# A two-layer transformer kernel on one core: the order of the value projection and of the query and key projections inside an attention slot

## The chip, the cores and the metric

The kernel runs on one core of one Trainium2 chip. The metric is device time in microseconds (us) of the whole program, lower is better. Engines are called PE (TensorE), DVE (VectorE), ACT (ScalarE), POOL (GpSimd) and SP (SyncE, which here only issues DMAs).

## The reference, cut to what matters

Eight sequences of 512 tokens with 256 features go through four blocks, each followed by a residual sum and a layer norm. The change touches only the first block's code; the routing part of the second runs in the same slots.

```
x = norm(x + attention_0(x))    # 16 heads of 16, softmax over keys j >= i
x = norm(x + experts_0(x))      # top 2 of 8, 7 experts of 512 slots, one no-op
x = norm(x + attention_1(x))    # rms norm, rotary, sigmoid weights divided by their sum
x = norm(x + experts_1(x))      # top 2 of 12, 8 experts of width 512, 4 that pass x on

# attention_0
q, k, v = split(x @ w_qkv + b_qkv)
s = where(j >= i, (q @ k.T) * 0.25, -inf)
out = softmax(s) @ v @ w_out + b_out
# experts_0, routing
w = softmax(x @ router_w.T + router_b); top 2; rank of each token in its expert, first 512 kept
```

## The kernel before, in words

The program has five stages: attention and routing of layer 0 (functions a_sp, a_pe, a_act, a_dve, a_pool), the experts of layer 0, attention and routing of layer 1, the experts of layer 1, and the last norm. A stage of attention is a software pipeline over the eight sequences. It is cut into ten slots, called zeroth, first, second, body (five times), seventh, eighth and ninth. In a body slot s the projections of sequence s+1 are made, the values and the row maxima of sequence s, the attention of sequence s-1, and output projection, norm and routing of sequence s-2.

A slot is a list of small steps, made once by `spread_out` at build time. Every engine walks the same list in order and does its own part of each step, and semaphores join them. So the list is the order of the instructions on every queue, SP's and POOL's too. The steps that matter here:

- `st n`, `av n` (20 each): scores of one unit (PE), exp (ACT, L834), mask of diagonal units (POOL, affine select, L1161), weights times values (PE, L719). `oe`, `on` (4 each): the accumulator is copied (ACT), transposed (PE, L729), and divided by the sum of the weights into o_nat (DVE, L909 and L911).
- `mx n` (40): PE makes scores again in bf16 (L810) and DVE takes their row maxima (L1093). `mc` splits 32 maxima into three bf16 parts (DVE, L1104 to L1108), `mr` turns them (PE, L819), `ms` stores them as three more rows of Q (SP, L667). `mc 0`, `mr 0`, `ms 0` stand in the middle of a slot, `mc 1` at its end, and `mr 1`, `ms 1` for it near the start of the next slot. Scores of the second half (`st 10`) wait for `ms 1`.
- `oT` (2): PE transposes o_nat (L737), ACT copies. `y` (2): output projection (PE, L745), residual sum (DVE, L921). `ln` (23 pieces): layer norm of y into x_out (DVE). `rT`, `lg`: PE transposes x_out (L755) and makes the router's logits (L762).
- `l1` (3 pieces), `l2` (22), `l3` (11): the routing, small DVE operations of 4 to 64 columns, each of which waits for the one before it. The first of l2 is L1004. `ps`: two small matmuls between l2 and l3. `sc` (8): POOL scatters the rows of x_out by indirect DMA (L1171).
- `qk n` (4): query and key projection of 128 columns for the next sequence. PE makes it (L793), ACT copies it twice out of the bank (L856, L861). `qs n`: DVE subtracts and casts (L1069, L1072), POOL subtracts once more (L1149), SP writes the three bf16 parts to DRAM (L650). `st_q 0` and `st_q 1` (SP, L603 and L607) load them back, stacked, for the first and the second eight heads. mx 0 of the next slot waits for the first stack, mx 20 for the second. qk come in the order 0, 2, 1, 3, where 0 and 2 belong to the first stack.
- `v n` (2): value projection of sequence s (PE, L800), bias and store by DVE (L1077). `xt` loads the transposed rows of sequence s+1 into the tile that v reads, and waits for v 1.

Three PSUM banks ("shared") are handed out in turn to every step of the list among xT, qk, ro, v, on, oT, y, rT, lg, ps, mx, mr (`bank_keys`). A step on PE therefore waits until the bank used three such steps before has been read, by DVE or by ACT.

How the list comes about: `evenly` merges two lists, the maxima and `rest`, so that both advance alike by the weights in WEIGHT (mx 0.9, v, y and qk 1.5, qs 0.8, rT 0.6, ln and each routing piece 0.25). Then the loop at the end of `spread_out` spreads the merged list over the st and av steps by the same weights. `("space", 0)` entries weigh 0.3 and vanish later.

## Time and profile before

| | us |
|---|---|
| median of 3 runs | 1785.55 |
| lowest, highest | 1783.24, 1787.79 |
| the profiled execution, its own time | 1787.79 |
| its span in the trace | 1786.0 |
| busy PE, DVE, ACT, POOL | 1456.3, 965.4, 694.6, 498.1 |
| mean granted clock of PE | 0.89 of full |

Busy times are sums over an engine's instructions. PE's includes time at the low clock. The body slots of layer 0 lie between about 147 and 492 us of the span, each between one oT 0 and the next.

### The profile page before, as it was taken

The numbers are of one execution on the slowest core, as the hardware profiler recorded it, in microseconds if no ns is written. First come the engines' busy times: TensorE is split into PE (matmuls) and PEld (weight loads), VectorE is DVE, ScalarE is ACT, GpSimd is POOL, SyncE is SP. The second block draws the span as 40 slices with busy tenths as digits, with TensorE's granted clock in tenths as the row PEclk, the third lists the DMA queues.
The fourth block names the chain that finished last, engine by engine and source line by source line (L and its number), as shares of the span: only waits on it lengthen the run. The fifth ranks groups of instructions, "written<-read, shape, count | busy, mean of one in ns | idle before, by whom it ended". The sixth has DMA issues, their size and how long they took to land.

```text
span 1786.0 us, 31302 instructions
## 1 busy us (share of the span) xinstructions
PE 1456.3 (82%) x10329; PEld 962.5 (54%) x10330; DVE 965.4 (54%) x3689; ACT 694.6 (39%) x957; POOL 498.1 (28%) x422
## 2 busy tenths in 40 slices
PE   3698898898798649999469999999998539999970
PEld 1245454454454426666235555565555429999970
DVE  3667778878866411111367776866653434444424
ACT  1153444454445311111045666666576312222222
POOL 4022233333334212121111132122212144444430
PEclk7798899999978669999689999999999769999995
DMA  6754336336333043432154534643635324444448
GB/s 160 195 115 88 83 92 141 88 92 137 87 61 107 13 160 86 127 95 59 35 119 99 107 77 105 132 110 71 128 84 146 133 75 72 71 71 71 69 82 250
DMA packets 122239, 182.88 MB, mean 102 GB/s; under 512 B 17112, under 2 KB 104562, under 8 KB 114433
## 3 DMA queue, kind: packets, MB, share of 16 engines
q1 hardware_dynamic: 98336, 151.84, 34.2%
q0 software_dynamic: 21504, 27.76, 9.6%
q10 hardware_dynamic: 2272, 1.67, 0.3%
q8 instruction: 70, 1.15, 0.3%
q14 instruction: 57, 0.46, 0.1%
HBM read 111.47 MB, written 77.02 MB: 106 GB/s over the span
## 4 chain that ended last, share of the span: by engine, by line
PE 57%; DVE 19%; issue 6%; DMA 5%; ACT 3%; POOL 1%; SPq 1%; DVEq 0%; ACTq 0%; POOLq 0%
PE ST L1795 7%; PE shared L1807 7%; PE ST L701 6%; PE OT L719 6%; PE ST L1261 6%; DVE scratch L1093 5%; PE shared L745 4%; PE OT L1269 3%; PE shared L1269 3%; PE shared L1456 2%; DMA x_in<-sum 2%; PE shared L793 2%; PE shared L810 2%; PE shared L762 2%; PE shared L737 2%
## 5 line engine op out<-in xcount | busy, mean ns | idle before, releaser
L834 ACT ACTIVATE arena<-ST 128x1024 f32<-128x1024 f32 x416 | 414.8, 1024 | 272.6 <-PE ST L701 267.4
L1093 DVE CUSTOM_DVE_ANT_0 scratch<-shared,mask 128x512 bf16<-128x512 f32 (+3 forms) x512 | 229.8, 486 | 92.6 <-PE shared L810 71.3
L701 PE MATMUL ST<-arena 96*128 96x256 bf16 (+2 forms) x1792 | 251.8, 277 | 15.3 <-DMA arena<-qk_parts 14.1
L719 PE MATMUL OT<-arena,v_aug 128*32 128x256 f32 (+1 forms) x3584 | 252.0, 383 | 4.1 <-POOL arena L1161 2.4
L701 PEld LDWEIGHTS ST<-arena 96*128 96x128 bf16 (+1 forms) x1792 | 159.9, 102 | 116.0 <-issue 50.6
L810 PE MATMUL shared<-arena 96*128 96x512 bf16 (+3 forms) x512 | 126.2, 322 | 52.7 <-DMA arena<-qk_parts 22.2
L1904 POOL DMA_INDIRECT sum<-arena,block_to_row x72 | 111.3, 1546 | 169.4 <-ACT arena L1858 157.8
L719 PEld LDWEIGHTS OT<-arena,v_aug 128*32 128x32 f32 x3584 | 85.1, 111 | 118.1 <-issue 66.4
L1161 POOL TENSOR_SCALAR_AFFINE_SELECT arena<-arena 128x512 f32<-128x512 f32 (+1 forms) x96 | 78.9, 822 | 226.0 <-ACT arena L834 226.0
L1807 PE MATMUL shared<-arena 128*128 x576 | 136.1, 379 | 0.0
L1636 POOL DMA_INDIRECT slot_x<-x_out,row_to x64 | 63.7, 995 | 177.0 <-DVE keep L1549 159.9
L810 PEld LDWEIGHTS shared<-arena 96*128 96x128 bf16 x512 | 43.4, 102 | 128.5 <-issue 65.1
L1807 PEld LDWEIGHTS shared<-arena 128*128 128x128 f32 x576 | 103.9, 190 | 11.2
L1621 POOL TENSOR_TENSOR qk_src<-qk_rest,qk_src 128x512 bf16<-128x512 f32 x32 | 37.7, 1178 | 252.0 <-DVE qk_src L1590 252.0
L1261 PE MATMUL ST<-arena 128*128 128x512 f32 x224 | 99.5, 603 | 5.1 <-ACT arena L1280 5.1
L1872 DVE COPY arena<-shared 128x256 f32<-128x256 f32 x72 | 30.5, 424 | 117.0 <-PE shared L1785 117.0
L1324 POOL DMA_INDIRECT sum<-arena,b_to x28 | 43.2, 1544 | 179.5 <-DVE arena L1307 151.6
L793 PE MATMUL shared<-xT,w_qkv 128*128 128x512 f32 x128 | 71.9, 694 | 24.7 <-DMA xT<-in_xT 14.6
L1290 DVE TENSOR_SCALAR arena<-ST 128x512 f32<-128x512 f32 x28 | 19.4, 691 | 111.2 <-PE ST L1261 111.2
L1171 POOL DMA_INDIRECT slot_x<-x_out,row_to x64 | 62.6, 979 | 50.3 <-DVE row_to L970 32.5
L1858 ACT ACTIVATE arena<-shared,block_gain 128x256 f32<-128x256 f32 x72 | 34.1, 474 | 106.4 <-PE shared L1807 106.4
L1852 ACT ACTIVATE arena<-ST 128x512 f32<-128x512 f32 x71 | 42.4, 597 | 84.7 <-PE ST L1795 84.7
(208 smaller groups left out, 2394.1 us busy)
## 6 DMA issues: line engine op xcount, KB each, us to landing
arena<-qk_parts SPq DMA_DIRECT2D x224, 128.0 KB, 7.2
qk_parts<-qk_src SPq DMA_DIRECT2D x64, 384.0 KB, 2.6
arena<-qk_parts SPq DMA_DIRECT2D x32, 384.0 KB, 4.6
block_rows<-slot_x SPq DMA_DIRECT2D x72, 130.0 KB, 2.2
arena<-qk_parts SPq DMA_DIRECT2D x32, 256.0 KB, 5.4
sum<-x_out SPq DMA_DIRECT2D x16, 512.0 KB, 2.9
arena<-in_experts_inter SPq DMA_DIRECT2D x7, 1024.0 KB, 5.2
arena<-in_experts_out SPq DMA_DIRECT2D x7, 1024.0 KB, 9.4
```

The costliest lines, as they stand in the source:

```text
L701: mm = pe.matmul(ST[n % 2][:, i * 256 + at:i * 256 + at + nq], K[par][0:rows, h, kb * P:(kb + 1) * P], Q[par][0:rows, h, q0:q0 + nq], star ...
L719: mm = pe.matmul(OT[32 * i:32 * i + 32, q0:q0 + nq], v_aug[par][:, kb, g * GH + i, :], PT[n % RING][:, i, at:at + nq], start=(u == 0), sto ...
L793: mm = pe.matmul(bank[:, :], w_qkv[:, c, n * P:(n + 1) * P], xT[:, c, :], start=(c == 0), stop=(c == CD - 1))
L810: mm = pe.matmul(bank[:, at:at + S - qb * P], Q[par][0:SK, head, qb * P:(qb + 1) * P], K[par][0:SK, head, qb * P:S], start=True, stop=True)
L834: act.activation(PT[n % RING][:, :, :], ST[n % 2][:, :].rearrange("p (h n) -> p h n", h=GH), func, scale=ATT_SCALE).then_inc(L["exp"], 1)
L1093: taken = dve.tensor_tensor_reduce(out=junk[n % 2][:, at:at + m], in0=bank[:, at:at + m], in1=mask[:, 0:m], scale=1.0, scalar=LOW, op0=ALU ...
L1161: pool.affine_select(out=v, in_=v, compare_op=ALU.is_ge, fill=0.0, base=0, pattern=[[0, GH], [0, blocks], [-1, P]], channel_multiplier=1). ...
L1261: mm = pe.matmul(up_banks[m % 4], wi[par][:, c, m * P:(m + 1) * P], xgT[:, c, :], start=(c == 0), stop=(c == CD - 1))
L1269: mm = pe.matmul(down_banks[t // 2][:, (t % 2) * D:(t % 2 + 1) * D], hT[:, m, t * P:(t + 1) * P], wo[par][:, m, :], start=(m == 0), stop=( ...
L1795: mm = pe.matmul(UP[par][:, f * P:(f + 1) * P], w1_now[par][:, c * F1 + f * P:c * F1 + (f + 1) * P], bxT[par][:, c * P:(c + 1) * P], start ...
L1807: mm = pe.matmul(Y_BANK[par][:, 0:D], bhT[par][:, c * P:(c + 1) * P], w2t[:, bass.ds(e * 1024 + c * D, D)], start=(c == 0), stop=(c == KF ...
L1904: pool.indirect_dma_start(out=sum1, out_offset=bass.IndirectOffsetOnAxis(ap=b_to_row[:, i:i + 1], axis=0), in_=by[i % 2], in_offset=None, ...
```

## The change

The projections of the next sequence, which stood in six places between the routing pieces, stand in two: four steps and st_q 0 between route_1 and route_2, and four steps behind the scatters. The value projections, which stood among the norm pieces, stand at the head of the list, before mr 1, ms 1 and oT. The load of the transposed rows (`load[1:]`) stands behind 12 norm pieces instead of 10. Weights, steps and the work of each step stay. The maxima that are merged in stay as they were. The lists of the slot "first" come out unchanged.

```diff
+NORM_FIRST = 12
+
 LATE = ("late", 0)
...
-        load, project = [], [[]] * 6
+        load, halves = [], [[], []]
         if ahead:
             load = [("xl", 0), ("xt", 0)] + ([("zr", 0)] if kind == "first" else [])
-            project = [[("qk", c[0])], [("qk", c[1]), ("qs", c[0])], [("qs", c[1]), ("st_q", 0)], [("qk", c[2])],
-                       [("qk", c[3]), ("qs", c[2])], [("qs", c[3])]]
-        rest = (start + y + norm[0:5] + [("v", 0)] + norm[5:10] + [("v", 1)] + load[1:] + norm[10:] + save + load[0:1]
-                + rows + route_1 + project[0] + route_2[0:6] + project[1] + route_2[6:12] + project[2] + route_2[12:] + project[3]
-                + route_3[0:9] + project[4] + route_3[9:] + project[5] + scatter)
+            halves = [[("qk", c[0]), ("qk", c[1]), ("qs", c[0]), ("qs", c[1]), ("st_q", 0)],
+                      [("qk", c[2]), ("qk", c[3]), ("qs", c[2]), ("qs", c[3])]]
+        rest = ([("v", 0), ("v", 1)] + start + y + norm[0:NORM_FIRST] + load[1:] + norm[NORM_FIRST:] + save + load[0:1]
+                + rows + route_1 + halves[0] + route_2 + route_3 + scatter + halves[1])
         others = evenly(maxima, rest, WEIGHT)
```

## Rows read from the trace of the kernel before

**Rows 1.** Windows, one body slot: busy us (count) by engine, clock, DMA.

```profile
219.70:287.70 68.00, 57.50 (x462) 33.48 (x463) 53.48 (x224) 31.37 (x41) 24.53 (x25) 0.93 0.46 108
```

**Rows 2.** Windows, two parts of a body slot: PE, PEld, DVE, ACT, POOL.

```profile
256.89:287.55 30.66, 22.80 (x198) 10.75 (x193) 27.70 (x115) 13.42 (x17) 10.45 (x11) 0.98 0.45 94
287.55:313.01 25.46, 22.89 (x168) 15.09 (x169) 19.03 (x81) 11.34 (x15) 9.98 (x11) 0.89 0.60 155
```

**Rows 3.** Instructions in order of time, DVE: start us, us, line, [idle before].

```profile
256.89 0.18 DVE L1004 TENSOR_REDUCE r_s<-r_w 128x4 f32<-128x32 f32 x1
...
277.35 1.06 DVE L965 TENSOR_TENSOR r_oh<-r_oh,r_c 128x64 f32<-128x64 f32 x1
...
279.16 0.56 DVE L1093 CUSTOM_DVE_ANT_0 scratch<-shared,mask 128x384 bf16<-128x384 f32 x1
...
279.85 0.69 DVE L1069 TENSOR_TENSOR qk_rest<-qk_flat,qk_src 128x512 f32<-128x512 f32 x1
...
280.92 0.42 DVE L1093 CUSTOM_DVE_ANT_0 scratch<-shared,mask 128x256 bf16<-128x256 f32 x1
...
285.21 1.15 DVE L1105 SCALAR_TENSOR_TENSOR mx_rest<-mx,mx_parts 128x32 f32<-128x32 f32 x1
...
287.13 0.42 DVE L911 TENSOR_TENSOR o_nat<-shared,o_sum 128x256 f32<-128x256 f32 x1
...
293.81 0.69 DVE L921 TENSOR_TENSOR y_b<-shared,x_res 128x512 f32<-128x512 f32 x1 [2.65 <-PE shared L745]
```

**Rows 4.** Instructions in order of time, PE, merged runs of one line.

```profile
252.63 1.88 PE L793 MATMUL shared<-xT,w_qkv 128*128 128x512 f32 x4
...
262.86 0.64 PE L719 MATMUL OT<-arena,v_aug 128*32 128x256 f32 x8
263.43 0.39 PE L810 MATMUL shared<-arena 96*128 96x256 bf16 x2
263.66 0.60 PE L701 MATMUL ST<-arena 99*128 99x256 bf16 x4
...
284.54 0.39 PE L810 MATMUL shared<-arena 96*128 96x512 bf16 x1 [1.40 <-DMA arena<-qk_parts]
286.91 0.48 PE L819 MATMUL shared<-ident_b,mx_parts 128*32 128x128 bf16 x3 [1.98 <-issue]
287.70 2.03 PE L737 MATMUL shared<-ident,o_nat 128*128 128x128 f32 x8 [0.32 <-DVE o_nat L911]
...
313.01 0.69 PE L755 MATMUL shared<-ident,x_out 128*128 128x128 f32 x4 [1.51 <-DVE x_out L938]
```

**Rows 5.** Instructions in order of time, POOL, end of a body slot.

```profile
277.24 1.10 POOL L1161 TENSOR_SCALAR_AFFINE_SELECT arena<-arena 128x1024 f32<-128x1024 f32 x1 [1.52 <-ACT arena L834]
...
285.17 1.15 POOL L1149 TENSOR_TENSOR qk_src<-qk_rest,qk_src 128x512 bf16<-128x512 f32 x1 [2.93 <-DVE qk_src L1072]
286.47 0.98 POOL L1171 DMA_INDIRECT slot_x<-x_out,row_to  x1 [0.15 <-issue]
...
295.44 0.97 POOL L1171 DMA_INDIRECT slot_x<-x_out,row_to  x1 [0.30 <-issue]
```

**Rows 6.** Instructions in order of time, ACT: the first copy of a projection.

```profile
261.19 0.69 ACT L856 ACTIVATE qk_src<-shared,b_qk 128x512 bf16<-128x512 f32 x1 [2.22 <-PE shared L793]
```

**Rows 7.** Instructions in order of time, SP: the second stack's first loads.

```profile
289.14 1.30 SPq L603 DMA_DIRECT2D arena<-qk_parts  x3
```

**Rows 8.** Windows of 4 us, columns as in rows 1 and 2.

```profile
266.00:270.00 4.00, 2.19 (x26) 0.91 (x24) 3.85 (x14) 2.56 (x3) 1.37 (x2) 1.00 0.21 75
548.00:552.00 4.00, 2.29 (x29) 0.91 (x29) 3.57 (x19) 0.89 (x1) 1.10 (x1) 1.00 0.01 2
552.00:556.00 4.00, 3.19 (x31) 1.56 (x23) 3.74 (x23) 0.60 (x1) 0.00 (x0) 0.55 0.00 0
```

**Rows 9.** Windows, the same steps (rT 0 to qk 2) in two slots.

```profile
170.70:189.50 18.80, 18.12 (x113) 11.39 (x113) 8.74 (x43) 8.07 (x11) 4.80 (x5) 0.65 0.09 30
244.88:259.17 14.29, 13.61 (x113) 8.61 (x113) 8.83 (x43) 7.96 (x11) 4.80 (x5) 0.88 0.12 39
```

## Prediction

> **What bounds the kernel now.** I read the page first: PE is busy for 82% of the span, DVE for 54%, and the slices say that the change lies in the first third, the sixteen-head attention of layer 0. The table of windows then gives one steady slot of it, and there are five such slots ("body"): 68.0 us, PE 57.5 us busy, DVE 53.5 us, mean granted clock 0.93 [rows 1]. Neither engine is full, so the slot alternates between a stretch that DVE sets and a stretch that PE sets. The same view over two parts of one slot shows it: from the first softmax step of the router (l2 piece 0) to the last normalised output (on 3) DVE is busy 27.7 of 30.66 us and PE 22.8; from there to the transposes of the next rows (rT 0) PE is busy 22.9 of 25.46 us and DVE 19.0 [rows 2]. The third view is the list of instructions in order of time. At the join of two slots DVE ends on 3 at 287.55, and PE has stood since 283: mx 0 waited 1.40 us for the stacked Q and K, mr 1 1.98 us for the split maxima, oT 0 0.32 us for o_nat [rows 3, 4]. The clock is then low, and eight transposes take 2.03 us. Before rT 0 PE stands 1.51 us for x_out [rows 4].
>
> **What the change does to the order.** I worked the planner out by its weights. The steps and their lengths stay; three things move in a body slot. (1) v 0 and v 1 stand before mr 1, oT and y: st0 mx0 v0 mx1 st1 v1 mx2 mx3 mr1 ms1 st2 oT0 mx4 oT1 av0 y0 ... y1 st4, instead of st0 mx0 mr1 oT0 oT1. The norm chain (23 pieces) begins after av2, not after av0, and ends at the same place, behind mx14. (2) The first two projections come together: qk2 moves from behind on1 to just behind st12, and qs0, qs2, st_q0 come before all 22 l2 pieces. (3) qk1, qk3, qs1, qs3 come behind the eight scatters, at the slot's very end. l2 and l3 (33 pieces) now run with mx26 to mx35 alone between them. The slot "first" keeps its order, "second" moves only mr 1, "seventh" has part (1) alone.
>
> Unit costs, start to start: an mx step costs DVE about 0.66 us (a two-part one 0.69: 279.16 to 279.85), a qs 1.07 us (279.85 to 280.92), a small chained op 0.2 us (the first one is 0.18 long) [rows 3]. On PE a qk is 1.88 us at full clock, and I take the same for v and y, which have as many columns; an av goes on after 0.57 us (262.86 to 263.43), an mx of 2 x 256 columns after 0.23 us (263.43 to 263.66; I take 0.27, since most have more columns), and an st, by the same overlap of 0.16 us, after 0.60 - 0.16 = 0.44 [rows 4]. On ACT a qk is two copies of 0.69 us each [rows 6].
>
> **Parts 2 and 3, from l2 to on 3.** Old length 30.66 us [rows 2]. Start at qk0, 252.63 [rows 4]; ACT ends its two copies 1.4 us after each qk, and the bank is free only then. PE now does qk0, av9, mx20, mx21, st12, qk2 and reaches mx22 near 258.5; DVE has read mx21 near 257 and has no l2 piece to fill with. It then does mx22, mr0, mx23, on1, qs0, mx24, qs2, mx25, and l2 begins at 264.8. The old order would have this same work done at 263.85 (it has about 1.25 us of l2 done and one qs of 1.07 us open at 264.0). Term: +0.95 us.
> Next l2 and l3: 33 pieces (6.9 us), ten mx (6.6 us), on2 (0.6 us): 14.2 us of DVE, 9.3 us of PE, so DVE sets it. Here DVE ops sometimes stand behind POOL: L1105 took 1.15 us and ended with the POOL subtraction that ran from 285.17; L965 took 1.06 us under the affine select from 277.24 [rows 3, 5]. Both are near 0.2 us otherwise by the small ops around them. POOL's two late subtractions (qs1, qs3) now come after the scatters, behind this stretch. I take -2.1 us (0.96 + 0.85 and some 0.3 of smaller cases). Bounds: 0 if other selects collide instead, -2.8 if all go.
> The Trainium skill has this as a rule (SBUF — State Buffer, "SBUF: two separate sides"): VectorE and GpSimd share one exclusive port pair, and the loser is blocked for the whole instruction. The two rows agree with it. By it alone the scatters' descriptor writes could collide too, and the term would be nothing.
> Then the end. Let T be the end of l3. qk1 hides under l3. qk3 must wait until ACT has emptied qk1's bank (T+0.65) and for mx37 and av18: it runs T+0.95 to T+2.8. DVE is done with mx36 and mx37 at T+1.4 and idles 1.75 us until mx38; then qs1, mx39, qs3, mc1 (0.85), on3 end at T+8.1. Term: +1.75 us, less 0.35 us of old gaps. Sum of the stretch: +0.95 - 2.1 + 1.75 - 0.35 = +0.25 us.
>
> **Part 1, from on 3 to rT 0.** Old length 25.46 us [rows 2]. st0, mx0 and v0 now run while DVE still does mc1 and on3: PE's 3.7 us of waits at the join are filled. The stack is issued some 4 us earlier with qs2 earlier, so mx0's 1.40 us goes too. But this is not the slot's gain. DVE now gets y1 only at 12.45 us after on3 (v1, oT0, oT1, y0 and y1 on PE, with ACT's copy of oT between); it got it at 9.7 us (y 0 waited 2.65 us, and y 1 follows) [rows 3]. Then eight mx (5.3 us) and 23 norm pieces (6.2 us) must pass DVE: 11.5 us and 0.4 us of collisions, so x_out is ready at 24.4 us. Term: 24.45 - 25.46 = -1.0 us. The bound from above is that the whole wait of PE at the join is given back, -3.7 us; from below 0.
>
> **What lies beside.** POOL: eight scatters take 8 x 1.28 us (286.47 to 295.44 are the first and last) [rows 5]; queued behind them are now qs1, qs3, then the select for av2. They end near 4.6 us into the slot, and st2's weights come only then: no cost. SP: qs1 and qs3 are saved and st_q 1 issued some 6 us later than 289.14 [rows 7]; behind it in SP's queue are ms 1 (wanted by st10, 31 us into the slot) and xt. Both have over 10 us. Cost 0; if that cover were gone, 6 us a slot.
>
> **The clock.** This is the term that decides. The change gathers DVE-only chains. l2 and l3 now have PE at 9.3 of 14.9 us, for 15 us on end without a projection, and from y1 to x_out PE has some 6.9 of 12 us. The "seventh" slot shows such a stretch already: at 548 to 552 PE is busy 2.29 of 4 us at clock 1.00, and at 552 to 556 the granted clock is 0.55, the lower of its two levels (1.2 GHz of 2.4) for most of it [rows 8]. What a fall costs depends on what it meets. The same PE work, rT 0 to qk2, takes 18.80 us at clock 0.65 and 14.29 us at 0.88 [rows 9]: 4.5 us. Where DVE sets the pace it costs nearly nothing. I expect one fall in l2/l3, reaching qk1, qk3 in some slots, and one around rT 0 that comes earlier than today's; today's at the join goes (already in the -1.0). I take +2.5 us a slot, about half of 4.5; bounds -1 and +5.
> The Trainium skill says (TensorE: Matmul & The Clock Gate, "HAM oscillation — how this bites in real kernels") that bursts of matmuls with waits between them fall back to the low clock, and this rule speaks against the change: by it both gathered stretches would fall in every slot. The rows above agree that such stretches can fall; a full count of two falls by the measured 4.5 us would make +9 us a slot, more than I take, since most of it would lie under DVE.
>
> **Sum.** +0.25 - 1.0 + 2.5 = +1.75 us, five times: +8.75 us; "seventh" 0, "second" 0. The profiled execution took 1787.79 us (span 1786.0): 1796.5 us. It stands 2.24 us above the median of 1785.55, so 1794.3 us, and I say 1794.
>
> **Rivals.**
> A. *No clock loss.* The order works by its sums alone: (0.25 - 1.0) x 5 and -1 us in "seventh": -4.75 us, 1781. For it: at 266 to 270 PE was busy 2.19 of 4 us in a body slot and stayed at clock 1.00 [rows 8]. Against: the fall at 552 in the same view. 0.24.
> B. *The join is the bound.* The filled wait comes back whole, and with the clock held there: -3 us x 6, 1768 to 1773. For it: the wait is the largest of the slot. Against: DVE has 53.5 us of work in 68 and had no gap there. It decides once x_out comes over 2 us sooner after on3 than 25.46. 0.15.
> C. *Everything cancels*: half the clock term, 1786. 0.13.
> D. *A late stack or maxima row*: SP's 6 us delay reaches st10 or mx20, +3 us or more a slot: 1800 and above. Against: over 10 us of slack. 0.05.
> My forecast: 0.43.
>
> **How the numbers follow.** 0.3% (5.4 us) is about what this kernel's measurement can tell. Faster than 1780.2: B and 0.1 of A, 0.26 with a little of C. Slower than 1790.9: D and most of the forecast, 0.46. The rest, 0.28. The range that holds 8 in 10 goes from 1774 (between A and B) to 1803 (clock term 4.3 a slot); the forecast's own is 1788 to 1801.
>
> **What would show it.** Body slots of 69.8 us (from 68.0); PE's wait before mr 1 and mx 0 gone; L1105 back at 0.2 us; a DVE wait for mx 22 of about 1.7 us and one for mx 38; PE at clock 0.5 somewhere in l2/l3 or near rT 0. I am wrong if mean granted clock over body slots is not below 0.93, or if on3 to rT0 falls below 23 us.

## The result and the profile after

The changed kernel took 1810.42 us (median of 4, 1808.2 to 1813.23), the kernel before beside it 1784.39 (1781.16 to 1787.79): ratio 1.015, 95% interval 1.0114 to 1.0186. It is slower, and by more than the predicted range (1774 to 1803) holds. The profiled execution of it took 1827.05 us (span 1825.3, clock 0.876), 14 us more than the highest of these four; 22 other executions of it on record took 1803.67 to 1821.11 us. Its trace has waits that most traces lack, which section 3 takes up. Windows of it, in the columns of [rows 1, 2]: the body slot that ends at 298.63, then its parts from the end of on 3 to rT 0, from rT 0 to l2 piece 0, and from there to the end of on 3:

```profile
224.88:298.63 73.75, 62.88 (x462) 35.29 (x463) 53.69 (x230) 31.36 (x41) 26.45 (x28) 0.83 0.45 102
227.41:253.42 26.01, 22.69 (x169) 13.75 (x168) 18.71 (x81) 11.24 (x15) 6.54 (x8) 0.89 0.64 142
253.42:274.19 20.77, 18.51 (x151) 11.14 (x151) 13.17 (x52) 11.27 (x15) 7.04 (x7) 0.91 0.12 37
274.19:300.52 26.33, 21.03 (x140) 9.88 (x141) 20.17 (x96) 7.82 (x10) 12.52 (x13) 0.69 0.53 115
```

DVE is as busy as in [rows 1], the slot is 5.8 us longer and the clock is 0.83 instead of 0.93. The five body slots take 76.5 us in the mean; before they took 69.1, the first of them 72.7 and the other four 68.0 to 68.4. Below I count half clock, the time that a slot would have spent at the lower level to give its mean granted clock, as 2 x (1 - granted clock) x length: 28.5 us of a slot, 13.1 before. The view prints the clock to two digits, so such a sum is good to about 0.4 us.

In order of time, the lines that answer to [rows 3, 4, 6] at two places of that slot (PE, DVE, ACT):

```profile
253.42 1.09 PE L756 MATMUL shared<-ident,x_out 128*128 128x128 f32 x4 [0.85 <-DVE x_out L939]
...
267.44 0.42 DVE L1094 CUSTOM_DVE_ANT_0 scratch<-shared,mask 128x256 bf16<-128x256 f32 x1 [1.99 <-PE shared L811]
...
293.99 0.65 PE L720 MATMUL OT<-arena,v_aug 128*32 128x128 f32 x16
...
297.70 0.19 DVE L1106 SCALAR_TENSOR_TENSOR mx_rest<-mx,mx_parts 128x32 f32<-128x32 f32 x1
...
297.89 0.60 ACT L840 ACTIVATE oT_raw<-OT 128x512 f32<-128x512 f32 x1 [2.96 <-remote]
...
298.63 1.09 PE L730 MATMUL shared<-ident,oT_raw 128*128 128x128 f32 x4 [4.00 <-ACT oT_raw L840]
```

L1106 is back at 0.19 us, and DVE waits 1.99 us for mx 22: both as predicted. Not predicted is the end. PE's av 19 starts at 293.99 and takes 0.65 us, but ACT, which waits for nothing else, starts its copy at 297.89. "remote" is printed where no instruction near in time explains the release. The semaphore that ACT waits for is raised by PE alone, and the trace has its change at 297.87, 3.2 us after the last matmul of av 19. In the five slots on 3 waited 1.92, 4.00, 5.40, 4.01 and 6.87 us for ACT, 0.81 each before. I call this a late signal of PE: the matmul is over by the profile, and its semaphore changes later.

The slot "second" ended 8.6 us later (its on 3 starts at 149.95 instead of 141.36). SP and PE there, after and then before:

```profile
106.22 1.78 SPq L668 DMA_DIRECT2D arena<-mx_rows  x3
108.12 0.51 SPq L638 DMA_DIRECT2D xT<-in_xT  x1
...
112.01 3.75 PE L794 MATMUL shared<-xT,w_qkv 128*128 128x512 f32 x4 [6.31 <-issue]
```

```profile
97.26 1.79 SPq L667 DMA_DIRECT2D arena<-mx_rows  x3
100.42 0.40 SPq L637 DMA_DIRECT2D xT<-in_xT  x1
...
105.52 1.95 PE L793 MATMUL shared<-xT,w_qkv 128*128 128x512 f32 x4 [0.76 <-issue]
```

With v first, mr 1 and ms 1 of "second" fall behind mx 10, the load of xT stands behind ms 1 in SP's queue and leaves 7.7 us later, and qk 0 waits for it. The first trace of before is the earliest of all here, so the size is better read over all twenty traces, ten with each order of this slot: the load leaves at 105.4 to 110.2 us with v first and at 100.4 to 102.9 otherwise, qk 0 waits 6.2 to 6.7 us against 0.5 to 2.1, and on 3 comes at 149.2 us in the mean against 144.0. So the change costs about 5 us here, though the two first traces differ by 8.

### The profile page after: what moved, and what is told of

Read it like the earlier page. It is cut to its first block, busy times and chain, and to the rows that moved or that the text cites. A ratio compares the mean times of both kernels' runs of the same rounds, so it can differ in the third digit from the quotient of the medians.

```text
span 1825.3 us, 31302 instructions
## 1 busy us (share of the span) xinstructions
PE 1480.0 (81%) x10329; PEld 968.2 (53%) x10330; DVE 957.6 (52%) x3689; ACT 693.6 (38%) x957; POOL 498.8 (27%) x422
## 4 chain that ended last, share of the span: by engine, by line
PE 56%; DVE 17%; issue 7%; DMA 5%; ACT 4%; POOL 1%; another core or an unknown queue 1%; SPq 1%; DVEq 0%; ACTq 0%; POOLq 0%
PE ST L1796 7%; PE shared L1808 7%; PE ST L702 6%; PE OT L720 6%; PE ST L1262 6%; DVE scratch L1094 4%; PE shared L746 3%; PE OT L1270 3%; PE shared L1270 3%; PE shared L794 2%; PE shared L1457 2%; DMA x_in<-sum 2%; PE shared L811 2%; PE shared L763 2%; PE shared L801 2%
## 5 line engine op out<-in xcount | busy, mean ns | idle before, releaser
L702 PE MATMUL ST<-arena 96*128 96x256 bf16 (+2 forms) x1792 | 258.3, 282 | 15.3 <-DMA arena<-qk_parts 13.2
L720 PE MATMUL OT<-arena,v_aug 128*32 128x256 f32 (+1 forms) x3584 | 261.5, 394 | 4.1 <-POOL arena L1162 2.7
L702 PEld LDWEIGHTS ST<-arena 96*128 96x128 bf16 (+1 forms) x1792 | 161.8, 104 | 119.8 <-issue 50.9
L811 PE MATMUL shared<-arena 96*128 96x512 bf16 (+3 forms) x512 | 133.0, 340 | 54.7 <-DVE mx L1094 26.4
L811 PEld LDWEIGHTS shared<-arena 96*128 96x128 bf16 x512 | 45.6, 105 | 136.7 <-issue 60.9
L1808 PEld LDWEIGHTS shared<-arena 128*128 128x128 f32 x576 | 103.9, 190 | 11.2
L1291 DVE TENSOR_SCALAR arena<-ST 128x512 f32<-128x512 f32 x28 | 19.4, 692 | 112.7 <-PE ST L1262 112.7
L922 DVE TENSOR_TENSOR y_b<-shared,x_res 128x512 f32<-128x512 f32 x32 | 22.1, 692 | 106.6 <-PE shared L746 71.4
L1172 POOL DMA_INDIRECT slot_x<-x_out,row_to x64 | 63.9, 999 | 46.7 <-DVE row_to L971 28.8
L730 PE MATMUL shared<-ident,oT_raw 128*128 128x128 f32 x256 | 48.0, 319 | 34.0 <-ACT oT_raw L840 18.9
```

Of the source, the lines that this page charges most:

```text
L702: mm = pe.matmul(ST[n % 2][:, i * 256 + at:i * 256 + at + nq], K[par][0:rows, h, kb * P:(kb + 1) * P], Q[par][0:rows, h, q0:q0 + nq], star ...
L720: mm = pe.matmul(OT[32 * i:32 * i + 32, q0:q0 + nq], v_aug[par][:, kb, g * GH + i, :], PT[n % RING][:, i, at:at + nq], start=(u == 0), sto ...
L811: mm = pe.matmul(bank[:, at:at + S - qb * P], Q[par][0:SK, head, qb * P:(qb + 1) * P], K[par][0:SK, head, qb * P:S], start=True, stop=True)
L1808: mm = pe.matmul(Y_BANK[par][:, 0:D], bhT[par][:, c * P:(c + 1) * P], w2t[:, bass.ds(e * 1024 + c * D, D)], start=(c == 0), stop=(c == KF ...
```

## The experiments

Eighteen runs were made, on four chips, each beside the kernel before on the same chip: 15 (the first four rows), 8 (the next four), 6 (the next four and the last two) and 7. This table is read first. "Slot" is the mean in us of the five body slots, from PE's start of on 3 to the next, in the one profiled execution, "half" the mean half clock in one; "late" tells whether the trace has waits over 1 us that end "remote".

| kernel | ratio (95%) | before beside it | slot | half | late |
|---|---|---|---|---|---|
| v_first_alone | 1.0142 (1.0067-1.0217) | 1802.97 | 74.2 | 14.2 | yes |
| halves_alone | 1.0109 (1.0036-1.0182) | 1802.97 | 75.6 | 25.9 | yes |
| after_maxima_first | 1.0121 (1.0048-1.0195) | 1802.97 | 76.1 | 26.8 | yes |
| after_half_before_scatter | 1.0244 (1.0165-1.0324) | 1802.97 | 80.1 | 29.0 | yes |
| before_again | 1.003 (0.9993-1.0066) | 1804.15 | 74.5 | 23.2 | yes |
| before_no_scatter | 0.9859 (0.9791-0.9927) | 1804.15 | 68.2 | 11.2 | layer 1 only |
| after_no_scatter | 1.0127 (1.0059-1.0194) | 1804.15 | 78.4 | 31.0 | layer 1 only |
| after_plain_store | 1.0125 (1.0047-1.0204) | 1804.15 | 75.6 | 23.1 | layer 1 only |
| v_first_no_scatter | 1.0032 (1.0017-1.0048) | 1783.78 | 70.5 | 12.3 | no |
| halves_no_scatter | 1.0016 (0.9995-1.0037) | 1783.78 | 73.0 | 23.1 | no |
| after_filled_no_scatter | 1.0126 (1.0084-1.0168) | 1783.78 | 73.4 | 7.8 | no |
| after_filled | 1.0168 (1.0122-1.0214) | 1783.78 | 73.7 | 12.6 | no |
| first_pair_no_scatter | 0.9978 (0.9956-1.0) | 1781.85 | 71.1 | 19.4 | no |
| second_pair_no_scatter | 0.9984 (0.9958-1.001) | 1781.85 | 71.5 | 16.1 | no |
| before_filled | 0.9997 (0.9975-1.0018) | 1781.85 | 70.2 | 13.2 | no |
| v_first_filled | 1.0138 (1.0067-1.0209) | 1781.85 | 75.2 | 21.6 | no |
| after_again | 1.0137 (1.0115-1.0159) | 1785.22 | 73.3 | 21.8 | no |
| before_filled_norm | 0.9992 (0.9979-1.0005) | 1785.22 | 68.7 | 11.3 | no |

Kernels named "no_scatter" leave layer 0's eight scatters out, so that the experts of layer 0 read empty rows, and are compared by slots; their ratios hold that omission too (it made the kernel before 0.9859 of itself where signals are late). Slots are compared on one chip where that can be done, since traces of one and the same program differ by 7 us a slot (section 3), and the kernel before by 20 us in all between these chips.

### 1. One half of the change at a time

```diff
 v_first_alone (projections as before)
-        rest = (start + y + norm[0:5] + [("v", 0)] + norm[5:10] + [("v", 1)] + load[1:] + norm[10:] + save + load[0:1]
+        rest = ([("v", 0), ("v", 1)] + start + y + norm[0:12] + load[1:] + norm[12:] + save + load[0:1]
 halves_alone (values as before)
+                + rows + route_1 + halves[0] + route_2 + route_3 + scatter + halves[1])
```

> The kernel before with one part of the change: v 0 and v 1 at the head of the list (and 12 norm pieces ahead of xt), projections where they were. Theory S (a queue): in the slot second, mr 1 and ms 1 now follow mx 10, and the load of the turned rows (xt) stands behind ms 1 on SP's queue; qk 0 waited 6.31 us for it in the changed kernel. That costs about +6 us once, here too. Theory V (join filled): each body slot and seventh gain 1 to 4 us. Theory C (the clock is lost only with the gathered projections): no further loss here. S with V gives 1773 to 1785 us; if the whole +25 us came with v, 1805 or more.

> The kernel before with the other part alone: projections in two halves, v and mr 1 where they were. Theory C (clock and balance): the loss of the body slots is all here, +2 to +4 us a slot, 1795 to 1805 us, and slot second is as before. Theory E (ACT's last copy oe 3 before on 3 comes late when scatters run at the slot's end): on 3 waits 2 to 6 us longer in the slots 2 to 6, as in the changed kernel's profile; then up to 18 us more. If the rival (the gathered v is what costs) holds, this is within 5 us of 1785.

Each half alone came out near the whole change (ratios 1.0142 and 1.0109, with intervals of 0.007 either way; the 1.015 of both was measured elsewhere, beside a kernel before of 1784). v first alone has the 6.28 us wait of qk 0 in "second", and halves alone waits 1.1 us there: v first brings the wait. But v first alone kept the clock (0.91 to 0.93 in three slots) and still took 75 us a slot. DVE's and ACT's waits at its join, with PE's steps that they wait for:

```profile
303.96 0.39 PE L810 MATMUL shared<-arena 96*128 96x384 bf16 x2
304.22 0.66 PE L737 MATMUL shared<-ident,o_nat 128*128 128x128 f32 x4
...
308.22 0.56 DVE L1093 CUSTOM_DVE_ANT_0 scratch<-shared,mask 128x384 bf16<-128x384 f32 x1 [4.05 <-remote]
```

A theory of the order alone has no place for a matmul of 0.39 us whose reader starts 3.9 us after it ended.

### 2. Two repairs of the changed order

```diff
 after_maxima_first: mr 1 and ms 1 ahead of v, oT and y behind it
-        rest = ([("v", 0), ("v", 1)] + start + y
+        rest = ([p for p in start if p[0] != "oT"] + [("v", 0), ("v", 1)] + [p for p in start if p[0] == "oT"] + y
 after_half_before_scatter
-                + rows + route_1 + halves[0] + route_2 + route_3 + scatter + halves[1])
+                + rows + route_1 + halves[0] + route_2 + route_3 + halves[1] + scatter)
```

> The changed kernel with mr 1 and ms 1 put back ahead of v 0 and v 1 (only oT and y stay behind v). Theory S: the 6.31 us wait of qk 0 in slot second goes, and the kernel takes 6 to 8 us less than the changed one, about 1803 us. If S is wrong (xt late for another reason), the wait stays. PE now waits for mc 1 before v 0 again, some 1 to 2 us a slot, so the rival gives 1810 or more.

> The changed kernel with the second half of the projections ahead of the eight scatters in the list. PE, DVE and ACT keep nearly their order (ACT and PE have no part in the scatters); POOL does its two subtractions before the scatters. Theory E: ACT's copy before on 3 then no longer comes late, on 3 waits 0.8 us in every slot, and the profiled execution loses some 18 us of its 1827. Theory P (POOL's order costs something else): the time falls by under 3 us and the late copies stay. If only clock and balance count: 1808 to 1812, no change.

The first gave "second" back (on 3 at 142.98 us instead of 149.95, qk 0 waits 0.5 us), so the place of ms 1 ahead of the load is shown as the cause of that wait. It gave nothing else: body slots of 76.1 us. The second took the wait of on 3 away (0.93 us), as its theory E said, and yet lengthened the kernel instead of shortening it, with slots of 74 to 84 us: the scatters now run behind the join, on 3 to rT 0 took 30.2 to 31.8 us in four slots, and late signals fell there. The wait moved with the scatters.

### 3. Are the late signals the order's?

before_again is the kernel before, unchanged. The two no_scatter kernels make the same replacement, and after_plain_store sends the same bytes without row indices:

```diff
-                        pool.indirect_dma_start(
-                            out=slot_x0, out_offset=bass.IndirectOffsetOnAxis(ap=row_to[par][:, t, i:i + 1], axis=0),
-                            in_=x_out[par][:, t, :], in_offset=None, bounds_check=E0 * CAP - 1,
-                            oob_is_err=False).then_inc(L["scattered"][par], 16)
 no_scatter
+                        pool.sem_inc(L["scattered"][par], 16)
 after_plain_store
+        spare = dram("spare", [24 * P, DX])
...
+                        pool.dma_start(spare[bass.ds(((k % 3) * 8 + t * 2 + i) * P, P), :],
+                                       x_out[par][:, t, :]).then_inc(L["scattered"][par], 16)
```

> The kernel before, unchanged, profiled once more. In the traces so far PE's signals arrive late at the join of two slots in all five kernels whose order was changed (a weights-times-values group that starts at 294.36 is signalled at 297.87, and ACT's copy of the accumulator waits 2.96 us), and in the first trace of the kernel before this does not occur once in 1786 us. Theory L (late signals): they need an order in which PE runs dry while the eight scatters are being issued; the order of before avoids it. Then this trace again has no wait over 1 us that ends with such a late signal, the body slots are 68.0 to 68.7 us, and the wait before on 3 is 0.81 us in each. Rival X (execution, not order): late signals belong to the execution or the chip, and the first trace of before merely had none. Then this trace has them too, also in the attention of layer 1, and its body slots are 69 us or more. The ratio to before is 1.00 by both.

> The kernel before with the eight scatters of layer 0 left out of every slot (POOL only raises their semaphore by as much), so layer 0's experts read empty rows. The reference for the next kernel. Theory L: before has no late signals to lose, and POOL's queue is not its bound, so a body slot keeps 67.5 to 68.3 us and the ratio is 0.993 to 1.000 (slots seventh and eighth may lose 1 or 2 us). Rival P (POOL's queue is the bound of the join in both kernels): slots of 66 us and less, ratio below 0.993.

> The changed kernel without the eight scatters of layer 0, with the same omission as the kernel before it in this list. Its waits before on 3 were 1.92, 4.00, 5.40, 4.01 and 6.87 us, 18 us above 0.81 each. Theory L: PE's late signals come only while scatters are issued. Then all five waits are at most 2 us, body slots fall from 76.5 to 71.5 to 73 us, and the ratio to before falls from 1.015 to 1.002 to 1.007; what is left is the clock (0.80 to 0.83 in body slots instead of 0.93) and the 6 us of slot second. Rival C (clock only; the wait before on 3 is an effect of ACT or PE being late by themselves): the waits stay at 4 us and more and the ratio stays at 1.011 to 1.017.

> The changed kernel in which each of the eight scatters of layer 0 is a plain DMA from POOL's queue of the same rows of x_out to a spare area (layer 0's experts read empty rows). Same bytes (130 KB each), but no row indices. Theory L with the packets as cause (DMA traffic of rows out of SBUF delays PE's signals): waits before on 3 of 3 to 7 us remain in most slots, ratio 1.011 to 1.017. Theory L with POOL's making of descriptors as cause: the waits go with the indirect instructions, at most 2 us each, ratio 1.002 to 1.008, if the plain DMA costs POOL clearly less than 0.97 us; if POOL takes as long for it, the waits stay and the two are not told apart.

My theory L, that the changed order makes them, fell at once. The kernel before has them too, on this chip. PE, ACT and DVE at its join, then windows of the slot and of its parts from on 3 to rT 0, rT 0 to l2, l2 to on 3:

```profile
304.35 0.60 PE L701 MATMUL ST<-arena 99*128 99x256 bf16 x4
304.85 1.99 PE L745 MATMUL shared<-w_o,oT 128*128 128x256 f32 x8
...
307.77 2.02 ACT L834 ACTIVATE arena<-ST 128x1024 f32<-128x1024 f32 x2 [5.25 <-remote]
308.54 0.69 DVE L921 TENSOR_TENSOR y_b<-shared,x_res 128x512 f32<-128x512 f32 x1 [2.44 <-remote]
```

```profile
292.51:367.62 75.11, 63.57 (x463) 36.71 (x463) 53.26 (x225) 31.45 (x41) 24.51 (x26) 0.84 0.42 98
298.00:324.38 26.38, 22.93 (x169) 14.97 (x169) 18.88 (x81) 11.32 (x15) 9.96 (x11) 0.89 0.60 149
324.38:340.81 16.43, 16.36 (x102) 10.48 (x103) 6.66 (x31) 6.72 (x10) 4.08 (x3) 0.61 0.09 32
340.81:373.10 32.29, 24.37 (x198) 11.25 (x193) 27.71 (x115) 13.42 (x17) 10.46 (x11) 0.92 0.43 90
```

Four slots of 75.1 us stand against 68.1 in the first trace. The part in which the late signals lie, on 3 to rT 0, is only 0.9 us longer; rT 0 to l2 takes 16.43 us at clock 0.61 instead of 12.02 at 0.86, and l2 to on 3 1.6 us more. Without scatters on the same chip the slot is that of the first trace again, to 0.01 us:

```profile
280.98:349.13 68.15, 57.65 (x462) 33.40 (x463) 53.41 (x225) 31.44 (x41) 16.69 (x18) 0.92 0.43 94
```

and the changed order lost its late signals in layer 0, but no time (the same view, after_no_scatter):

```profile
307.48:385.99 78.51, 68.10 (x463) 37.63 (x463) 53.30 (x225) 31.42 (x41) 16.68 (x17) 0.78 0.38 82
```

So the loss isn't made of late signals: with the scatters out on one chip, the change costs 10.4 us in this slot and 48 us in all (1824.93 against 1776.58). That misses theory L's 71.5 to 73 us a slot and its ratio of 1.002 to 1.007; 1.0127 is what its rival C said. DVE is busy for the same 53.3 us; PE runs at clock 0.78. The 10.4 us is no fixed price of the order either: section 6 finds 4 to 5 us a slot with the scatters in, on another chip. The plain stores, which take POOL 4.28 us for eight where the scatters take 10, gave no late signal in layer 0, while layer 1, whose scatters stay, has them in the same trace; the ratio stayed at 1.0125, above the 1.002 to 1.008 expected.

### 4. Clock or order? Doubled matmuls as filler

```diff
-                        for of_pair, qb, at in FILLS[n % len(FILLS)]:
+                        for of_pair, qb, at in FILLS[n % len(FILLS)] * (2 if turn.kind == "body" and (9 <= n <= 15 or 24 <= n <= 35) else 1):
```

PE makes the scores of these maxima twice into the same bank. v_first_no_scatter and halves_no_scatter are the kernels of section 1 without scatters.

> The kernel before with only the value projections at the head of the list, and without layer 0's scatters. With the scatters left out PE's late signals are gone in layer 0, so this shows the order by itself; the reference is the kernel before without scatters (slots 68.15 us, 1776.58 us, ratio 0.986, half clock for about 10.9 us of a slot). Theory C (what the change costs is the low clock that comes with the gathered projections): v first alone keeps the clock, body slots of 67.5 to 69.5 us, ratio 0.984 to 0.991 (6 us of it from xt behind ms 1 in slot second). Rival V (v first costs time by itself, since DVE gets y 1 later): slots of 71 us and more, ratio above 0.995.

> The kernel before with only the query and key projections in two halves, and without layer 0's scatters. Theory C: this half of the change carries the loss: half clock for 25 us or more of a slot, body slots of 75 to 79 us, ratio 1.005 to 1.013. Rival (both halves of the change are needed together for the low clock): slots below 72 us, ratio below 0.998.

> The changed kernel without layer 0's scatters, in which PE makes the scores of maxima 9 to 15 and 24 to 35 of a body slot twice into the same bank (19 steps of about 0.27 us, 5.1 us more work a slot, no other step moved). They lie in the two stretches where DVE sets the pace and PE is busy for 2.2 to 2.8 of 4 us. Theory C: the clock is the cause of the 78.5 us slots, and work that keeps PE busy keeps it up. Half clock falls from 31 us to under 18 us a slot, slots fall to 70 to 74 us and the ratio from 1.013 to 0.99 to 1.003, although PE does more. Rival W (the low clock is a symptom; the slot is long because of what waits for what): more work can only lengthen it, slots of 78.5 us and more, ratio 1.013 or above.

> The changed kernel with the same doubled maxima 9 to 15 and 24 to 35, scatters in place, the whole output made. Theory C: half clock under 20 us a slot instead of 25 to 32, slots of 71 to 76 us (late signals at the join still cost some), ratio 0.998 to 1.009 instead of 1.015. Rival W: 1.015 or above.

The ratios of the first three came out against a kernel before of 1783.78, not of 1804, so the expected ones don't apply; the slots do. For after_filled they do apply: 1.0168 is outside theory C's 0.998 to 1.009 and is what rival W said. v first kept the clock in the middle slots (68.4, 67.7, 69.0 us) and lost it in the first and the last (72.3, 75.0). Halves took 76.6, then 71.7 to 72.5, 73.0 in the mean, which neither its theory (75 to 79) nor its rival (below 72) had said. One slot of each, then after_filled_no_scatter (slot, then its three parts):

```profile
291.00:358.67 67.67, 56.96 (x463) 31.97 (x463) 53.02 (x225) 31.28 (x41) 16.69 (x18) 0.95 0.44 95
```

```profile
292.72:364.58 71.86, 61.58 (x462) 35.19 (x463) 53.69 (x225) 31.37 (x41) 16.67 (x17) 0.83 0.41 89
```

```profile
296.44:368.17 71.73, 60.10 (x492) 33.30 (x493) 54.15 (x225) 31.27 (x41) 16.66 (x17) 0.98 0.42 90
301.43:326.38 24.95, 21.14 (x175) 12.81 (x175) 19.05 (x80) 11.23 (x15) 3.13 (x4) 1.00 0.63 120
326.38:347.65 21.27, 19.75 (x158) 10.94 (x158) 13.07 (x50) 11.31 (x15) 7.00 (x7) 0.92 0.11 36
347.65:373.15 25.50, 19.22 (x160) 9.54 (x160) 22.01 (x96) 8.72 (x12) 6.52 (x7) 1.00 0.48 105
```

The filler held the clock: half clock fell to 7.8 us a slot, and the middle slots run at 0.98. Against section 3's slot PE is busy for 8 us less (68.10 to 60.10) with 5 us more of work, and the slot is 6.8 us shorter. But those two ran on different chips, and that difference can't be put down to the filler. On the filler's own chip the changed kernel without it has slots of 70.9 to 75.8 us (section 6), 73.3 in the mean at 21.8 us of half clock; the two filled kernels have 73.4 and 73.7 at 7.8 and 12.6. So the clock came back and no time with it, in the slots or in the whole (1.0168 against 1.0137 without filler, and the intervals overlap). Whether what the clock gave was eaten by the filler's own work, this can't tell. At clock 0.98 the slot is still 71.7 us, 3.6 more than before, and the added time lies between rT 0 and on 3 (46.8 us against 42.7): that much is the order's or the filler's, and not the clock's.

What the clock does cost is seen best where PE alone sets the pace. From rT 0 to qk 0 in two slots of after_filled, the same PE work takes 6.6 us at full and 11.5 us at half clock:

```profile
401.70:408.31 6.61, 6.47 (x63) 4.66 (x64) 4.22 (x20) 3.14 (x4) 4.05 (x3) 1.00 0.24 82
471.57:483.05 11.48, 11.48 (x64) 8.21 (x64) 4.92 (x24) 3.36 (x5) 4.08 (x3) 0.50 0.17 48
```

### 5. Which pair, and does filler help the order before?

first_pair gathers qk 0, qk 2, qs 0, qs 2, st_q 0 ahead of l2 alone; second_pair moves the other four behind the scatters' place alone. Both leave the scatters out as in section 3. The last three are whole kernels with the filler of section 4 for other n; v_first_filled has the edit of v_first_alone too.

```diff
 first_pair_no_scatter
+                + rows + route_1 + project[0] + project[1] + project[2] + route_2 + project[3]
 second_pair_no_scatter
+                + route_3 + scatter + project[3] + project[4] + project[5])
 before_filled, v_first_filled, before_filled_norm
+ 9 <= n <= 15 or n >= 33
+ 9 <= n <= 15
+ 9 <= n <= 15
```

> The kernel before with only the first pair gathered (qk 0, qk 2, qs 0, qs 2 and st_q 0 ahead of all l2 pieces; qk 1 and qk 3 where they were), without layer 0's scatters. Read by the stretch from qk 0 to on 3, which is 29.44 us before and 34.23 to 34.46 us with both pairs moved. Theory G (DVE starves while PE makes two projections close together and DVE has no routing pieces to do): the first pair costs +2.5 us (DVE waits 3.0 and 2.0 us there instead of 1.6 and 0.8): 31.5 to 32.5 us, slots of 70 to 71.5 us. Rival E (the pair at the end does it): 29.4 to 30.2 us.

> The kernel before with only the second pair moved (qk 1, qk 3, qs 1, qs 3 behind the scatters' place), without layer 0's scatters. Theory G: DVE has nothing but mx left there and waits about 1.9 us before mx 38 plus what l3 hid: qk 0 to on 3 takes 31 to 32 us, slots of 70 to 72 us. Rival E: 33.5 us or more, all of the loss. If the two kernels' surpluses add up to about 4.9 us, the pairs act independently.

> The kernel before, whole, in which PE makes the scores of maxima 9 to 15 and 33 to 39 of a body slot twice (14 steps, 3.8 us more PE work a slot, where it has gaps). Theory C: half clock per slot falls from 10.9 us (or 24 us, where PE's late signals had stretched the join) to under 7 us, slots become 66 to 68 us where no late signal falls, ratio 0.985 to 0.998. Rival W: the added work lies on PE's path from qk 0 to on 3 and costs 1 to 2 us a slot, ratio 1.003 to 1.008.

> The kernel before, whole, with the value projections first and the scores of maxima 9 to 15 of a body slot made twice (7 steps, 1.9 us of PE). Theory C: the fall before rT 0, which costs 3.7 us when it covers rT 0 to qk 0 (11.5 us instead of 7.8), goes; slots of 66.5 to 70 us, plus the late signals at the join; ratio 0.995 to 1.005. Rival V: late signals hit this order harder, since PE runs dry behind av 0 with oT waiting; slots of 73 us and more, ratio 1.01 and above.

> The kernel before, whole, in which PE makes the scores of maxima 9 to 15 of a body slot twice (7 steps, 1.9 us of PE). With maxima 33 to 39 doubled too, rT 0 to qk 0 fell from 7.8 to 6.6 us and qk 0 to on 3 grew from 29.4 to 32 to 33.6 us. Theory C: without the latter, rT 0 to qk 0 stays 6.6 us and qk 0 to on 3 goes back to 29.4 to 30 us: slots of 66.7 to 67.5 us, ratio 0.995 to 0.999. Rival W: the low clock only moves (to qk 0, or to the join) and slots stay 68 us or more, ratio 0.999 to 1.004.

From qk 0 to on 3 the first pair alone took 32.6 to 33.0 us and the second alone 32.2 to 33.7, from 29.4; both together 34.0 to 34.6 (halves_no_scatter, the four slots after the first). Each costs about 3 us and they don't add up. Rival E, that the pair at the end does it all, is out, since the first pair alone costs as much. The sizes are a miss: 2.5 and about 2 us were expected. A middle slot of each:

```profile
285.81:357.50 71.69, 61.20 (x462) 35.16 (x463) 54.01 (x225) 31.59 (x41) 16.71 (x18) 0.86 0.40 90
```

```profile
285.92:356.10 70.18, 58.63 (x463) 34.18 (x463) 53.96 (x225) 31.26 (x41) 16.69 (x17) 0.90 0.40 92
```

before_filled made rT 0 to qk 0 6.6 to 6.8 us (7.8 before), as expected, and lost more behind qk 0 (37.3 to 39.0 us to the end of on 3, 34.9 before), where PE is the late one and its doubled maxima lie on the path, at a lower clock too (0.89 to 0.92 for 0.98). before_filled_norm leaves those out and still gained nothing: the low clock moved behind qk 1 (2.9 us of it before qk 3, where there was none), and the slots stayed at 68.3 to 68.5 us, the last 69.9. Rival W was right there. v_first_filled was the clearest miss: 75 us a slot with 11.5 us of half clock between rT 0 and qk 0, no late signal and no gain. Its rival V had the number, but by late signals, of which there were none. Filler of 1.9 us a slot didn't hold the clock. None of these beats the kernel before by what a measurement can tell.

### 6. The changed kernel once more, without late signals

> The changed kernel, unchanged, profiled and timed once more, on the chip that times the kernel before beside it. Theory H (late signals belong to the chip): layer 0 and layer 1 either both have them or both have none. If none: on 3 waits about 0.9 us in every body slot, qk 0 to on 3 takes 34 to 36.5 us, slots are 71.5 to 78.5 us by how far the low clock reaches (rT 0 to qk 0 either 7.6 or 11.5 us), and the ratio is 1.010 to 1.020 with before near 1783. Theory L (they come with the order): they are in layer 0 but not in layer 1.

What theory H said held: no late signal in either layer. One trace on a chip that had shown none before is a weak test of it. The ratio is 1.0137, with slots of 73.9, 70.9, 71.5, 74.5 and 75.8 us. The third of them and its three parts:

```profile
294.31:365.78 71.47, 60.99 (x462) 32.96 (x463) 51.80 (x225) 31.38 (x41) 25.46 (x26) 0.88 0.47 105
297.83:322.36 24.53, 19.84 (x163) 11.96 (x164) 18.63 (x81) 11.25 (x15) 6.55 (x8) 1.00 0.72 151
322.36:343.63 21.27, 18.88 (x151) 10.34 (x151) 13.06 (x50) 11.39 (x15) 7.00 (x7) 0.92 0.11 35
343.63:369.30 25.67, 22.27 (x148) 10.67 (x148) 20.11 (x96) 8.74 (x11) 11.75 (x13) 0.73 0.52 117
```

The last part again in the fourth slot, where less of it ran at half clock, and in the last slot of after_filled, at full clock with 12 doubled maxima in it:

```profile
418.89:443.76 24.87, 20.33 (x148) 9.47 (x148) 21.36 (x96) 8.74 (x11) 10.80 (x12) 0.86 0.51 114
496.82:521.22 24.40, 19.22 (x160) 9.54 (x160) 20.56 (x96) 8.73 (x12) 11.16 (x12) 1.00 0.50 96
```

The third slot's instructions in order of time, DVE, PE and POOL:

```profile
329.90 2.54 PE L794 MATMUL shared<-xT,w_qkv 128*128 128x512 f32 x4
...
333.50 0.69 DVE L1094 CUSTOM_DVE_ANT_0 scratch<-shared,mask 128x512 bf16<-128x512 f32 x1 [3.09 <-PE shared L811]
...
336.89 0.42 DVE L1094 CUSTOM_DVE_ANT_0 scratch<-shared,mask 128x256 bf16<-128x256 f32 x1 [1.99 <-PE shared L811]
...
340.95 1.15 POOL L1150 TENSOR_TENSOR qk_src<-qk_rest,qk_src 128x512 bf16<-128x512 f32 x1 [1.09 <-DVE qk_src L1073]
...
341.47 1.18 DVE L1070 TENSOR_TENSOR qk_rest<-qk_flat,qk_src 128x512 f32<-128x512 f32 x1
...
343.63 0.18 DVE L1005 TENSOR_REDUCE r_s<-r_w 128x4 f32<-128x32 f32 x1
...
357.76 0.17 DVE L971 TENSOR_TENSOR row_to<-r_s 128x8 int32<-128x8 f32 x1
...
358.52 1.98 PE L794 MATMUL shared<-xT,w_qkv 128*128 128x512 f32 x4
...
360.94 0.56 DVE L1094 CUSTOM_DVE_ANT_0 scratch<-shared,mask 128x384 bf16<-128x384 f32 x1 [2.10 <-PE shared L811]
...
364.28 0.69 DVE L1094 CUSTOM_DVE_ANT_0 scratch<-shared,mask 128x512 bf16<-128x512 f32 x1 [1.87 <-PE shared L811]
...
368.88 0.42 DVE L912 TENSOR_TENSOR o_nat<-shared,o_sum 128x256 f32<-128x256 f32 x1
```

and qk 1, the end of l3 and mx 38 in the fourth:

```profile
431.79 1.98 PE L794 MATMUL shared<-xT,w_qkv 128*128 128x512 f32 x4
...
434.28 0.17 DVE L971 TENSOR_TENSOR row_to<-r_s 128x8 int32<-128x8 f32 x1
...
438.73 0.69 DVE L1094 CUSTOM_DVE_ANT_0 scratch<-shared,mask 128x512 bf16<-128x512 f32 x1 [1.92 <-PE shared L811]
```

## Why the prediction was wrong, step by step

All by after_again, where no late signal disturbs the reading. The forecast had the direction. Two of its steps failed: the +0.25 us for parts 2 and 3 of a body slot, and the 0 for the slot "second".

- **Part 1, on 3 to rT 0: right in four slots.** Predicted 24.45 us; 24.53 in three slots, 24.88 in the fourth, and 27.79 in the first (25.3 before). PE's wait before mr 1 is 0.44 us (1.98 before) and that before mx 0 is gone (1.40), DVE's late y 1 took the gain as worked out, and PE stands 1.52 us for x_out as before. With the first slot the five gained 0.2 us each in the mean, not 1.0.
- **Parts 2 and 3, predicted +0.25: this step failed.** From rT 0 to the end of on 3 the slots took 46.4 and 46.9 us, and 49.9 and 50.9, against 42.7 before: +3.7 and +4.3, and +7.3 and +8.2 (the first, 45.6, has to be read against 48.9). The sum had a slip as well: its own times, added from qk 0 to on 3, are 12.2 + 14.2 + 8.1 = 34.5 us, 0.45 less than the old 34.92 and not 0.25 more. The third slot took 39.4, 4.9 more than that:
  - l2 was to begin 12.2 us after qk 0 (252.63 to 264.8). It began 13.7 us after (329.90 to 343.63). I had one DVE wait of 1.75 us in mind; there are two, 3.09 us for mx 20 behind qk 0 (1.61 before) and 1.99 us for mx 22 behind qk 2. And the two gathered subtractions took 0.91 and 1.18 us, not 0.69.
  - l2 and l3 took 14.3 us (343.63 to 357.93) for a predicted 14.2.
  - Then the end. With T the end of l3 (357.93), "qk1 hides under l3", and mx 38 was to come at T + 3.15. qk 1 started at T + 0.6, DVE waited 2.10 us for mx 36 behind it and 1.87 for mx 38 behind qk 3, and mx 38 came at T + 6.35. From there to the end of on 3 it was 5.02 us for a predicted 4.95. So +3.2 us of the miss stands where the prediction hid qk 1.
  - Only a small part of that is the low clock, whose price in l2 and l3 I had taken as "nearly nothing". In the fourth slot, with 7 instead of 13 us of half clock there, qk 1 did start 2.7 us before l3 ended (431.79, T = 434.45), and the wait for mx 36 was gone. But l2 and l3 then took 15.6 us instead of 14.3, and mx 38 still came at T + 4.3 and not at T + 3.15. The part took 24.87 us for 25.67, so in this trace the clock is worth 0.8 us of it. With the filler and at full clock it took 24.1 and 24.4 us in after_filled, 25.50 without scatters: 0.2 to 1.6 us. Against the 22.3 us that the prediction's times give for this part, some 2 us (24.1 to 24.9) are lost even where qk 1 is hidden. There qk 3 holds PE while DVE has nothing left but a maximum that needs PE (1.92 us of waiting). How much an unfilled PE at full clock would have given was not tried.
- **The collisions, -2.1 us: right where I looked.** L1106 took 0.19 us and L966 0.22. But three new ones came: the two subtractions, +0.7 us, and L978, 1.17 us for 0.75 in before_no_scatter.
  The 1.18 us one ended 0.55 us behind POOL's subtraction (340.95 to 342.10), the 0.91 us one 0.55 us behind an affine select. The Trainium skill's rule that VectorE and GpSimd share one exclusive port pair (SBUF — State Buffer, "SBUF: two separate sides") agrees with both. What I forgot to ask of a moved step is what POOL does beside it in its new place.
- **The clock, +2.5: too much.** rT 0 to qk 0 took 11.5 us instead of 7.5 to 8.3 in two of five slots; before, it did so in one of five, so the mean grew by 0.8 us (8.5 to 9.3). The other fall, in l2 and l3, came in all five (6.7 to 13.7 us of half clock), at the 0.8 us above. Together that is some 1.6 us a slot, an estimate from these rows. The Trainium skill's rule that bursts with waits between them fall back (TensorE: Matmul & The Clock Gate, "HAM oscillation — how this bites in real kernels") named both stretches; l2 and l3 fell in all five slots, the stretch around rT 0 in two, and the slots came out 4.2 us longer in the mean, not the 9 that two full falls in each would make.
- **"second" 0: wrong.** I had costed the SP queue for the body slots alone, where xt keeps its cover. In "second" the same move puts ms 1 right ahead of it: +8.1 us between these two traces, about 5 over all twenty. after_maxima_first shows it by giving the time back.
- **"seventh" 0:** -4.3 us (63.9 from 68.15), with half clock 12.8 us instead of 25.9.

Sum to on 3 of slot eighth: 21.0 (body) + 8.1 - 4.3 = +24.8 us (621.66 from 596.90). The medians on that chip differ by 20.05. The rest of the program was 10 us shorter in this one execution than in the first trace of before; single executions of the kernel before spread over 12 us (1778.37 to 1790.13), so I read nothing into it.

Rival D had the right size and the wrong place: a late load on SP, but in "second", and the body slots lost time without one. The forecast's +1.75 us a slot was 4.2.

**What stays open.** The changed order takes 71 to 79 us a slot by how far the half clock reaches, with the same instructions. What decides that was not found: without scatters it was 78.5 us in three slots on end, with them, on another chip, 70.9 to 75.8. The first profiled execution of it had late signals and the four timed ones lay beside a kernel before of 1784; on which chip it ran is not on record. What makes PE's signals late was not found either.

## What to carry to other kernels

When steps are gathered, cost three things for the new place: what the engine that they leave has left to keep its clock, whether "hidden under" still holds if that engine runs at half speed, and what stands beside them on POOL. Walk every queue in every kind of slot, the rare ones first: one load behind one wait in one slot cost 5 to 8 us of 20. Two steps that hold one engine, one after the other, starve the other engine if the gathering has left it nothing else to do; check what is left there, too. Where the slot length hangs on the clock's pattern, a reordering is measured by profiles of several executions and by parts of the slot, since one trace can show 68 or 75 us for the same program. And a repair is compared with the unrepaired kernel on the same chip: the filler looked like a gain of 6.8 us a slot until that was done, and then like none.

## What the runs showed of the hardware

- **PE's signals can come 1 to 6 us late while POOL issues indirect DMAs.** All nine traces with such waits show them only there, inside a train of eight scatters, with the semaphore changing 1.0 to 6.1 us after the matmul's end: the changed kernel's first one and the eight from two of the chips. The other eleven have none, in either layer. On those two chips the kernel before took 1803 and 1804 us, on the other two 1782 to 1785. Leaving the scatters of layer 0 out took the waits of layer 0 away and gave the kernel before 1776.58; plain DMAs of the same bytes took them away too. That scatters are needed for them is shown; that the chip decides is what twenty traces agree on, not a test. It may also be the reason for the 1827.05 us of the first profiled execution, which was not tested.
- **Late signals go with a loss larger than their waits.** In before_again the part that holds them grew by 0.9 us and the slot by 7, since PE ran on at half clock (0.61 from rT 0 to l2). Both went when the scatters were left out on the same chip; that the late signals brought the half clock is inferred from this.
- **The same PE work, 6.6 us at full clock, takes 11.5 us at half clock** where PE alone sets the pace (section 4). From l2 to on 3, where DVE sets it for most of the way, 25.67 us with 13 us of half clock before the end of l3 stand against 24.87 with 7.
- **More matmuls can make PE less busy.** With 30 more instructions PE was busy for 60.10 us of a slot (clock 0.98), and for 60.99 without them on the same chip (clock 0.88). The slots were as long as without (71.73 and 71.47 us), and the same filler in smaller amounts (1.9 us a slot) did not hold the clock.
